# Decoder stage: self- and cross-attention batches in turns, cross-attention one round later, buffers doubled by parity

## The reference

```python
x_self = _prob_sparse_self_attn(x, self_out_w, self_out_b)   # 16 heads of 8; q = k = v = x
x = _layernorm(x + x_self, ln1_g, ln1_b)
x_cross = _mha_cross(x, memory, cross_in_w, ...)             # 77 context tokens
x = _layernorm(x + x_cross, ln2_g, ln2_b)
h = jax.nn.gelu(x @ ffn_w1.T + ffn_b1, approximate=False)
x = _layernorm(x + h @ ffn_w2.T + ffn_b2, ln3_g, ln3_b)      # and a norm of x + decoder(x)
...
u = max(1, int(math.ceil(math.log(L + 1))))                  # 5: largest scores kept in a row
_, idx = jax.lax.top_k(scores, u)                            # self-attention only
```

## Time and profile before

| | |
|---|---|
| median of 3 runs | 8549.72 us (8532.59 to 8566.16) |
| profiled execution | 8530.47 us, span 8528.5 us |
| busy shares of the span | PE 76%, PEld 40%, DVE 79%, ACT 51%, POOL 57% |
| mean granted TensorE clock | 0.844 |
| decoder stage in the span | 6388.7 to 8182.9 us |

### The profile page before, as it was taken

How to read it: one execution, slowest core, us unless ns; L and a number is a source line. 1 busy time by engine, 2 the same in 40 slices (tenths; PEclk the granted TensorE clock), 3 DMA queues, 4 the chain that set the end, 5 groups by cost and what they waited for, 6 DMA issues and landing times. The chain is left out here.

```text
span 8528.5 us, 94682 instructions
## 1 busy us (share of the span) xinstructions
PE 6482.7 (76%) x25859; PEld 3438.7 (40%) x25859; DVE 6736.4 (79%) x16402; ACT 4379.4 (51%) x8810; POOL 4872.2 (57%) x2829
## 2 busy tenths in 40 slices
PE   5888888888888888888788867777556777777755
PEld 2333333333333333333355535445434545545532
DVE  5999999999999999999755568888666766666657
ACT  3555555555555555555454523333325666666633
POOL 4888888888788888888644334444213333333310
PEclk8898898898998898888898878888657998888865
DMA  4333333333333333333300056666310000000011
GB/s 182 133 147 155 140 148 153 146 147 144 144 147 145 147 145 147 147 154 133 111 26 25 16 155 198 191 193 196 100 51 8 10 9 9 9 9 9 6 31 36
DMA packets 373737, 896.62 MB, mean 105 GB/s; under 512 B 28032, under 2 KB 270077, under 8 KB 306973
## 3 DMA queue, kind: packets, MB, share of 16 engines
q1 hardware_dynamic: 332508, 692.64, 21.7%
q0 software_dynamic: 40960, 201.36, 8.3%
HBM read 850.58 MB, written 56.77 MB: 106 GB/s over the span
## 5 line engine op out<-in xcount | busy, mean ns | idle before, releaser
L380 POOL TENSOR_TENSOR mb_dBu<-mb_dtu,mb_rows_b 128x1024 f32<-128x1024 f32 x1027 | 2406.7, 2361 | 358.0 <-DVE mb_bank L394 184.1
L394 DVE TENSOR_TENSOR_SCAN mb_bank<-mb_bank,mb_dBu 128x1024 f32<-128x1024 f32 x704 | 1612.2, 2290 | 71.5 <-PEq L63 50.8
L434 PE MATMUL mb_bank<-mb_hcd,ident 128*128 128x512 f32 x2560 | 1266.4, 622 | 72.7 <-DVE mb_hcd L408 72.7
L365 ACT ACTIVATE mb_bank<-mb_dt,mb_a_neg 128x508 f32<-128x508 f32 x2050 | 1310.6, 670 | 0.8
L434 PE MATMUL mb_bank<-mb_hcp,ident 128*128 128x512 f32 x1280 | 796.0, 755 | 370.7 <-POOL mb_hcp L417 370.7
L417 POOL TENSOR_TENSOR mb_hcp<-mb_hs,mb_rows_c 128x1024 f32<-128x1024 f32 x320 | 752.9, 2353 | 357.3 <-DVE mb_hs L394 353.5
L408 DVE TENSOR_TENSOR mb_hcd<-mb_bank,mb_rows_c 128x1024 f32<-128x1024 f32 x704 | 862.1, 1225 | 31.4
L1538 POOL DMA_INDIRECT ex_rows<-in_ex_table,ex_idx x512 | 490.5, 958 | 608.3 <-DVE ex_idx L1534 392.9
L434 PEld LDWEIGHTS mb_bank<-mb_hcd,ident 128*128 128x128 f32 x2560 | 500.6, 202 | 787.2 <-issue 587.7
L394 DVE TENSOR_TENSOR_SCAN mb_hs<-mb_bank,mb_dBu 128x1024 f32<-128x1024 f32 x320 | 730.8, 2284 | 40.9 <-ACT mb_bank L365 40.9
L434 PEld LDWEIGHTS mb_bank<-mb_hcp,ident 128*128 128x128 f32 x1280 | 283.6, 235 | 820.2 <-POOL mb_hcp L417 498.1
(11 more groups left out here) (368 smaller groups left out, 13495.0 us busy)
## 6 DMA issues: line engine op xcount, KB each, us to landing
mb_rows_b<-bc_rows SPq DMA_DIRECT2D x259, 1024.0 KB, 7.7
mb_rows_c<-bc_rows SPq DMA_DIRECT2D x258, 1024.0 KB, 6.9
stream<-mb_r_post SPq DMA_DIRECT2D x69, 256.0 KB, 2.4
mb_r_tok<-stream SPq DMA_DIRECT2D x67, 256.0 KB, 2.8
mb_r_post<-stream SPq DMA_DIRECT2D x65, 256.0 KB, 2.9
ex_rows<-in_ex_table,ex_idx POOLq DMA_INDIRECT x512
tj_x_tok<-stream SPq DMA_DIRECT2D x17, 256.0 KB, 3.1
bc_rows<-mb_xp SPq DMA_DIRECT2D x65, 64.0 KB, 1.6
```

The source lines that it names most:

```text
L365: e = nc.scalar.activation(da_of(n)[:, c * GB:(c + 1) * GB, 1:], dt[q][:, c].rearrange("p (b t) -> p b t", b=GB)[:, :, 1:], ACT.Exp, scale ...
L380: nc.gpsimd.tensor_tensor(by_c(dBu[m % RING][:]), by_c(chains(dtu[q][:])), over_c(rows_b[:, n]), ALU.mult).then_inc(s["mb_dbu"], 1)
L394: nc.vector.tensor_tensor_scan(flat(to), flat(da_of(n)), flat(dBu[n % RING][:]), 0.0, ALU.mult, ALU.add).then_inc(s["mb_scan"], 1)
L434: m = nc.tensor.matmul(bank[:, B_Y + c], ident[:], part[:, c * GB:(c + 1) * GB], start=False, stop=False)
```

## The change

Self and cross batches alternate in a round (self batch 0, cross batch 0, self batch 1, ...), so that the units are two self, two cross, two self and so on. Round i now works on the cross-attention of group i - 1 and the feed-forward of group i - 2; norm 1 and the q, k, v projections of group i stay in round i, and their results are read one round later. What is read in a later round (`xT`, `qT`, `kT`, `vself`, `vx`, `b_own`, `b_c`) has two buffers, chosen by the parity of the round. There are 20 rounds, and the loop body holds two of them (rounds 2 to 13, six times through). Small steps move within the round: the norm of `xn1` from steps 10 to 13 of one round to steps 0 to 2 of the next, `kT` behind it, the transposes of `xn1` from t = 0 to 3.

```diff
+    def place(self, n):
+        return (n // 2 if self.mixed else n) % GB
...
-            return [own if 0 <= i + 1 < GROUPS else None] * GB + [cross if 0 <= i < GROUPS else None] * GB
+            q = (i + 1) % 2
+            return [own[q] if 0 <= i + 1 < GROUPS else None, cross[q] if 0 <= i - 1 < GROUPS else None] * GB
...
-            has_own, has_cross, has_ffn = (0 <= shape + k < GROUPS for k in (1, 0, -1))
+            q = shape % 2
+            has_own, has_norm, has_ffn = (0 <= shape + k < GROUPS for k in (1, 0, -2))
...
                 def _(pool):
+                        if t == 1 and has_norm:
+                            n1.pool(pool)
...
-                        if t == 11 and has_own:
-                            n1.pool(pool)
-                        if t == 12 and has_next:
+                        if t == 8 and has_next:
                             pool.wait_ge(p["x"], 16)
...
+                            at.wait(pool, "added", -2)
+                            pool_next(pool, q)
...
                 def _(pe):
-                        if t == 0 and has_cross:
-                            for b in range(GB):
-                                m = nc.tensor.transpose(bank[:, L, b * P:(b + 1) * P], xn1[:, b], ident[:])
...
-                        if t == 2 and has_cross:
+                        if t == 2 and has_norm:
                             pe.wait_ge(p["ks"], 1)
                             for b in range(GB):
                                 m = nc.tensor.matmul(bank[0:NC, R, b * D:(b + 1) * D], cT[:, b], wv[:], start=True, stop=True)
                             m.then_inc(p["v"], 1)
+                        if t == 3 and has_norm:
+                            pe.wait_ge(p["n1_rows"], 1)
+                            for b in range(GB):
+                                m = nc.tensor.transpose(bank[:, L, b * P:(b + 1) * P], xn1[:, b], ident[:])
+                            m.then_inc(p["y1t"], 1)
+                        if t == 4 and has_norm:
+                            pe.wait_ge(p["y1s"], 1)
+                            nc.tensor.matmul(bank[:, L], wq[:], flat(yT), start=True, stop=True).then_inc(p["q"], 1)
...
                 def _(act):
+                        if t == 3 and has_norm:
                             act.wait_ge(p["y1t"], 1)
                             nc.scalar.activation(flat(yT), bank[:, L], ACT.Identity, scale=vecs[:, G1C:G1C + 1],
...
+                        if t == 2 and has_norm:
+                            n1.act(act, a1, xn1)
                             act.wait_ge(p["k"], 1)
-                            nc.scalar.activation(flat(kT), bank[:, R, 0:GB * NC], ACT.Identity, bias=vecs[:, BK:BK + 1]).then_inc(p["ks"], 1)
+                            nc.scalar.activation(flat(kT[q]), bank[:, R, 0:GB * NC], ACT.Identity, bias=vecs[:, BK:BK + 1]).then_inc(p["ks"], 1)
...
                 def _(dve):
-                        if t == 12 and has_cross:
-                            dve.wait_ge(p["bc"], 2)
+                        if t == 4 and has_norm:
+                            dve.wait_ge(p["n1_rows"], 1)
+                        if t == 6 and has_ffn:
+                            dve.wait_ge(p["n2_rows"], 1)
                         at.dve_step(dve, t)
+                        if t == 0 and has_norm:
+                            n1.dve_done(dve)
...
-        for i in (-2, -1, 0):
+        for i in range(-2, 2):
             round_of(i, i)
-        with nc.Fori(1, GROUPS - 2) as i:
-            round_of(i, 1)
-        for i in range(GROUPS - 2, GROUPS + 1):
+        with nc.Fori(0, (GROUPS - 4) // 2) as pairs:
+            for q in range(2):
+                round_of(pairs * 2 + 2 + q, 2 + q)
+        for i in range(GROUPS - 2, GROUPS + 2):
             round_of(i, i)
```

More of the change, by code:

```diff
@@ L995, in pool_step @@
         self.wait(pool, "score", 2 * n - 3)
[L996 removed]
+        self.nc.gpsimd.tensor_tensor(self.km[n % 2][:, :, 0:nk], kind.k(self.place(n)).unsqueeze(1).to_broadcast([P, H, nk]),
                                      self.hmask[:].unsqueeze(2).to_broadcast([P, H, nk]), ALU.mult).then_inc(self.sem("km"), 1)
@@ L1002, in pe_scores @@
         n, half = divmod(t, 2)
-        kind, b = self.batch(n), n % GB
+        kind, b = self.batch(n), self.place(n)
         self.wait(pe, "km", n)
@@ L1170, in dve_add @@
         self.wait(dve, "proj", n)
-        self.batch(n).add(dve, n % GB, self.bank[:, 7, P:P + D]).then_inc(self.sem("added"), 1)
-        self.batch(n).added(dve, n % GB)
+        self.batch(n).add(dve, self.place(n), self.bank[:, 7, P:P + D]).then_inc(self.sem("added"), 1)
+        self.batch(n).added(dve, self.place(n))
     def dve_step(self, dve, t):
@@ L2088, in sb, with two @@
             return st.enter_context(nc.sbuf_tensor("de_" + name, shape, dt))
+        def two(name, shape, dt=F32):
+            return [sb(f"{name}{q}", shape, dt) for q in range(2)]
         bank = st.enter_context(nc.psum_tensor("de_bank", [P, 8, 512], F32))
@@ L2132, in decoder_stage, with own_of, add, rows_of @@
-        cross = Kind(NC, DK ** -0.5, False, lambda b: qT[:, b], lambda b: kT[:, b], lambda b, h: vx[:, b, h], wo[:], add_cross, rows_cross)
+        at = Attend(nc, sb, p, "a", bank, ident, hmask, SEQ, True, mixed=True)
+        def own_of(q):
+            def add(dve, b, psum):
+                return nc.vector.tensor_tensor(a1[:, b], b_own[q][:, b], psum, ALU.add)
+            def rows_of(dve, b):
+                dve.drain()
+                n1.dve_rows(dve, a1, [b])
+            return Kind(SEQ, D ** -0.5, True, lambda b: xT[q][:, b], lambda b: xT[q][:, b], lambda b, h: vself[q][:, b, h], ws[:],
+                        add, rows_of)
@@ new lines, in cross_of, with add, rows_of @@
+        def cross_of(q):
+            def add(dve, b, psum):
+                return nc.vector.tensor_tensor(a2[:, b], b_c[q][:, b], psum, ALU.add)
+            def rows_of(dve, b):
+                dve.drain()
+                n2.dve_rows(dve, a2, [b])
+            return Kind(NC, DK ** -0.5, False, lambda b: qT[q][:, b], lambda b: kT[q][:, b], lambda b, h: vx[q][:, b, h], wo[:],
+                        add, rows_of)
+        own, cross = ([of(q) for q in range(2)] for of in (own_of, cross_of))
@@ L2290, in _ @@
                             m.then_inc(p["ct"], 1)
-                        if t == 1 and has_cross:
-                            pe.wait_ge(p["y1s"], 1)
-                            nc.tensor.matmul(bank[:, L], wq[:], flat(yT), start=True, stop=True).then_inc(p["q"], 1)
+                        if t == 1 and has_norm:
                             pe.wait_ge(p["cts"], 1)
                             nc.tensor.matmul(bank[:, R, 0:GB * NC], wk[:], flat(cT), start=True, stop=True).then_inc(p["k"], 1)
-                        if t == 2 and has_cross:
+                        if t == 2 and has_norm:
                             pe.wait_ge(p["ks"], 1)
```

111 lines of the change are left out of this document (44 added, 67 removed).

## The result

The changed kernel took 8740.53 us (median of 4 runs, 8738.86 to 8746.06), the kernel before 8551.27 us (4 runs, 8532.59 to 8566.16): ratio 1.0223, 95% interval 1.0203 to 1.0243. It is slower, by about 190 us. The forecast (8665 us, range 8575 to 8740) had the sign; its size is 75 us too small, so that the measured time lies half a microsecond above the range.

The account below looks back on a forecast made before the run. A latency chain, with no engine full, bounds the decoder round; 91.1 us of chain plus additions gave 108.1, with clock 114. Over 14 rounds and the ends that was +133 us on 8530.5, so 8665 us, range 8575 to 8740.

Parts of the forecast that it names:

- the steps of the chain: Decoder waits from one second self pick to the next: 22.8 us for a self and a cross batch, 91.1 a round.
- The keys step: ScalarE normalises four batches before writing kT, so its copy ends 1.7 us late; norm and keys together add 4.1 a round.
- the gap at the gelu: Expected sign: VectorE waits 3 us or more before the second pick of the self batch behind the gelu.
- the bank pair as the stall: Only one PSUM bank pair holds scores, so each of a round's four self-to-cross-to-self changes was said to stall.
- X: Length of a full decoder round after the change: 108.1 us at full clock plus 5.6, rounded 114; break-even 104.5.
- the one with the last norm: Period of a round where the last norm's rows run on VectorE in step 12, priced at +2.4 us.
- the feed-forward's term: w1 matmuls, bias activations and gelu ahead of self scores and exponentials add 6.8 us to a round.
- The branch: VectorE starts late behind the loop's branch back: 2.7 us less what it would have waited, 2.1 each.
- The clock: TensorE's granted clock taken as 0.91, not full, adding 5.6 us to each full round.
- Self batches without cross ones: Early decoder rounds: such a batch costs some 16.8 us; prologue and first rounds 101.5, round 0 78.
- Last rounds: Decoder's end: round 15 at 64 us, another cross-only round 61.1 and the last 44.6.
- Rival 1: Cross steps fall under VectorE's replace work: round 86 us, kernel 8271, half way 8426; chance 0.07 for anything faster by 0.5%.

Follow-up runs that it names:

- The two-by-two order: Changed kernel with two self batches, two cross batches, and again, in place of strict alternation; ratio 1.0051 to the kernel before, round 105.6 us.
- the kinds apart: Changed kernel with four self batches, then four cross batches in a round, all else kept; ratio 1.0022 to the kernel before, round 106.6 us.
- The eight transposes: Eight added identity transposes on TensorE ahead of its wait for each pick; ratio 1.0216 in the changed kernel, 0.9965 in the kernel before.
- the last variant of the kernel before: Kernel before with all rounds written out, negated maxima on ScalarE and eight added identity transposes ahead of each pick wait; ratio 1.0010.
- taking the tables away: Changed kernel with the gelu replaced by a plain copy, so without its two table loads; ratio 1.0203 to the kernel before, round 115.8 us.
- early scores with keys, maxima and no branch: Changed kernel with scores always early, kT ahead of norm 1, negated maxima on ScalarE and all rounds written out; ratio 0.9987 to the kernel before.

## Where the prediction was right, and which step failed

**Right.** The decoder became slower since alternation, with TensorE's order as it is, lengthens a full round, and the steps of the chain were those read from the kernel before, each within 0.05 us in the round shown. Most of what was to be seen is there: VectorE idle 2.40 ahead of MAX8 and 1.71 ahead of the second shift; wv waiting 1.28 for kT; DVE's share down from 934.40 / 1396.7 = 67% (rounds 1 to 13 before) to 886.28 / 1396.6 = 63%. The keys step was priced at 1.7 and measured 2.0. Two signs came short: the second picks are 26 to 32 us apart, not 23 to 30, and the gap at the gelu is 3.16 us in one round of twelve and 2.3 in the others, where 3 or more was to be seen.

**The step that failed: the bank pair as the stall.** "The single score bank pair makes each change of kind a stall" was the step that carried the forecast, and it is wrong as it stands. With one bank pair and all four changes, moving the scores ahead in TensorE's order gives 12.1 of the round back, and 9.0 of it at one place: self scores that stand behind values, projection and cross transposes. TensorE then waits 2.2 us of a round for the banks. The prediction named that order ("since the order puts scores behind the transposes") but for the cross scores, which are worth 1.2; ahead of the self scores it stood in the sum as 1.77 us and was taken as given. That the chain's sum came near the measured one couldn't tell the two causes apart; the runs did. The two-by-two order said the same from the other side. One thing wasn't run: scores always early with the kinds apart, or in the kernel before. So it isn't shown how much of the 12.1 us belongs to alternation and how much any order of batches would gain.

**The base.** I set 133 us on the profiled execution's 8530.5 and called 8664 the median, though I had seen the median 19 us higher. The median of the kernel before is 21 us above that execution: 21 of the 75 us. The stages ahead of the decoder, untouched, began it at 6388.7 in one profile and 6419.7 in the other.

**The terms that were too small.** The decoder has 184.9 - 133 = 52 us more than forecast; with the 21 of the base this is 73 of the 75 us.

- *Rounds 1 to 14*, X: 109.7 + 1396.6 + 109.9 = 1616.2 against 14 x 114 - 18 = 1578: +38. By the sum at full clock the period with norm and keys should take 22.8 + 4.1 = 26.9 us, the one with the gelu 29.6, the one with the last norm 25.2, and the one over the edge 25.7 in line and 27.8 behind the branch. They take 28.5 to 31.2, 29.7 to 30.2, 26.3 to 26.9, 27.8, and 30.7 to 32.2. So the feed-forward's term was near, and the others too small. The branch comes to 3 us or more in place of 2.1, and to 4.8 by the rounds written out, which would be 13 us of the 38. In the period with the keys the four scores of the second self half take 3.57 us in place of 1.88 where the clock is low (last section). In the one with the last norm VectorE's TENSOR_SCALAR takes 1.64 us at 7521.82 in place of 0.17, a wait that the sum had at nothing. How the rest divides isn't settled.
- *The clock*, 5.6 us of X: no run confirms this price. It came from two rounds of the kernel before, 103.6 us at 0.92 and 109.2 at 0.83. The eight transposes raised the clock by 0.07 and took 0.6 us off a round of the changed kernel, by 0.10 and took 1.4 off one of the kernel before, and in the last variant of the kernel before 109.2 us was also measured at 0.91. So X came as near as 114 to 116.4 partly by luck: a clock term that no run bears out as a whole stands in for chain terms that were too small by up to 116.4 - 108.1 = 8.3 us.
- *Self batches without cross ones*: prologue and rounds -2 to 0 took 201.2, not 179.5: +22. I had 5.4 us from the second pick to MAX8. The trace of round -1 has both picks in a row (L1152 x2) and then the whole TensorE path ahead of the scores (the second block is VectorE; its last line shows the first two of eight MAX8):

```profile
6476.10 1.97 PE L1032 MATMUL de_bank<-ident,de_a_e 128*128 128x128 f32 x8 [3.96 <-DVE de_a_e L1152]
6479.18 1.08 PE L1043 MATMUL de_bank<-de_a_pt,de_vself 128*32 128x128 f32 x16 [1.11 <-ACT de_a_pt L1106]
6480.19 1.97 PE L1032 MATMUL de_bank<-ident,de_a_e 128*128 128x128 f32 x8
6481.95 2.71 PE L1017 MATMUL de_bank<-de_a_km,de_xT 128*128 128x512 f32 x4
```

```profile
6474.81 2.36 DVE L1152 SCALAR_TENSOR_TENSOR de_a_e<-de_a_mr,de_a_e 128x1024 f32<-128x1024 f32 x2
6485.76 0.49 DVE L1137 MAX8 de_a_m<-de_a_sp 128x8 f32<-128x128 f32 x2 [8.59 <-ACT de_a_sp L1086]
```

VectorE is idle for 8.59 us, and from one batch's picks to the next it is 20.6 us and not 16.8. The two cross units between are empty, so the scores of the next self batch stand in TensorE's program behind the transposes of both picks and the values of the first.
- *Last rounds*: 61.3 + 54.9 + 45.5 = 161.7 against 169.7: -8.

**The gelu** was priced at 6.8 with its feed-forward. The period is 29.8, 22.8 + 7.0, so its place in the trace bears the number out. But taking the tables away saves 0.6 of a round, moving it costs 1.7 and with early scores its place is worth 0.3: what it stops is made up elsewhere. A wait that is on the chain at one point isn't a time that the round gives back.

**Rival 1**, that interleaving works, is not what this change does, and the best interleaved form is just ahead of the kernel before: early scores with keys, maxima and no branch, 0.9987. Its rounds are 5 us shorter than the 107.4 of the kernel before, and 1.8 shorter than the 104.2 of the kernel before with all rounds written out; one round more and self-only rounds of 82 us take that back. The plain kernel before with two rounds in the body is as fast or faster, 0.9964, for one edited loop. The Trainium skill (Perfetto Trace Analysis, Optimization Strategy) says that performance may be improved by interleaving regimes. Here the alternating round with early scores takes 104.3 us, against 106.6 apart with TensorE's order as it was, and no run shows a shorter kernel from it (1.0025 against 1.0022).

## What to carry to other kernels

When work is put into a new order, the rules that decide who goes first inside a step (here: scores ahead of or behind the transposes) were written for the old neighbours; look at each for the new ones before judging the order. Where an engine starts a matmul later than its banks are free, ask what stands ahead of it in the program, not what it shares. Price a term by the round that it gives back, not by the wait that it shows. Set a sum on the median of the runs, not on the one profiled. And look at more than one round: here the gap at the gelu was 3.16 us in one and 2.3 in eleven.

## What the runs showed of the hardware

A VectorE TENSOR_SCALAR of 8 elements, 0.17 us by itself, takes up to 1.89 us while GpSimd masks keys, and ends with it. VectorE and GpSimd at the start of a round:

```profile
7549.47 1.89 DVE L1140 TENSOR_SCALAR de_a_nb<-de_a_m 128x8 f32<-128x8 f32 x1
```

```profile
7547.73 3.61 POOL L1002 TENSOR_TENSOR de_a_km<-de_xT,hmask 128x2048 f32<-128x2048 f32 x1 [10.13 <-POOLq L63]
```

GpSimd ends at 7551.34, TENSOR_SCALAR at 7551.36; MAX8 beside the same mask is not slowed (1.65). Summed over the trace, this instruction takes 62.8 us for 96 in rounds 2 to 13, and 39.0 for 104 in rounds 1 to 13 of the kernel before. The Trainium skill (SBUF — State Buffer, Terms) says that VectorE and GpSimd share a port pair that one of them holds for its whole instruction; the trace agrees for this instruction, and MAX8 isn't held up by it.

TensorE's time for the same four score matmuls, those of the second self half behind wv, was 1.88 us in the round from 7431.0 (at 7459.43, granted clock 1.00 from 7459.4 to 7461.4) and 3.57 in the next one. There the granted clock was 1.00 from 7562.0 to 7572.5 and 0.53 from 7572.5 to 7576.1, so that most of the matmuls ran at the lower of the two levels, 1.2 GHz. TensorE had waited 1.60 and 1.28 us ahead of them in both rounds, so these two waits alone don't explain the fall:

```profile
7572.51 3.57 PE L1017 MATMUL de_bank<-de_a_km,de_xT 128*128 128x512 f32 x4
```

A loop's branch back seems to cost more than VectorE's late start of 2.7 us: seven fewer in the kernel before gave 30 us, some 4 each. Twelve fewer gave no more (28 us), so the price isn't the same for each. The Trainium skill (Runtime: NRT & Kernel Launch, Instruction fetch mechanics) says that a taken branch whose target is outside the fetched pages waits for a fetch. The runs agree with its direction; that the time is a fetch, no run here shows.
